# Last attention network: source logits of all heads transposed once and spread by identity columns

## What is computed

```python
ft = jnp.einsum('nhd,od->nho', hv, W)
a1 = jnp.sum(ft * attn_l, axis=-1)          # source logits, [1250, 12]
a2 = jnp.sum(ft * attn_r, axis=-1)          # destination logits
e = jax.nn.leaky_relu(a1[src] + a2[dst], negative_slope=0.2)
m = jax.ops.segment_max(e, dst, num_segments=n)
w = jnp.exp(e - m[dst])
denom = jax.ops.segment_sum(w, dst, num_segments=n)
alpha = w / jnp.maximum(denom[dst], 1e-16)
agg = jax.ops.segment_sum(alpha[:, :, None] * ft[src], dst, num_segments=n)
out = jax.nn.relu((agg + res).reshape(n, H * DOUT))
```

## Time and profile before

| what | value |
|---|---|
| median of three runs | 3462.98 us |
| lowest and highest run | 3449.34 and 3463.35 us |
| profiled execution, its own time | 3472.38 us |
| its span | 3470.6 us |
| PE busy, DVE busy, ACT busy in it | 3244.2, 2175.4, 1338.4 us |
| mean granted clock of PE | 0.951 of full speed |
| the last network, from the barrier to the end | about 3007 to 3470.6 us |

### The profile page before, as it was taken

One profiled execution on the slowest core, in us unless ns is written; L12 is line 12 of the kernel. 1 busy time (PEld: TensorE's weight loads), 2 busy tenths in 40 slices (PEclk: granted clock), 3 DMA queues, 4 the chain that ended last, 5 costly groups with the idle time before them and its releaser, 6 DMA issues. The chain is left out here.

```text
span 3470.6 us, 60801 instructions
## 1 busy us (share of the span) xinstructions
PE 3244.2 (93%) x20813; PEld 3037.5 (88%) x20813; DVE 2175.4 (63%) x4032; ACT 1338.4 (39%) x2526; POOL 944.3 (27%) x968
## 2 busy tenths in 40 slices
PE   6998998999998999999999999999998898899998
PEld 5887777888887999999997889999988686799998
DVE  6888646667677631018867601228877565499998
ACT  1245233323333121115446411124446330488885
POOL 1101733544555330005547300014546200000000
PEclk9988999999999999999998999999999889899997
DMA  3123344223222343337767633347767400300001
GB/s 80 35 81 117 121 123 117 59 73 104 55 56 67 85 135 121 102 126 244 238 208 229 177 123 101 101 143 243 242 199 233 143 33 15 73 1 0 0 0 45
DMA packets 160165, 386.02 MB, mean 111 GB/s; under 512 B 29619, under 2 KB 98784, under 8 KB 159959
## 3 DMA queue, kind: packets, MB, share of 16 engines
q0 software_dynamic: 47200, 173.39, 16.4%
q1 hardware_dynamic: 75274, 147.18, 14.4%
q10 hardware_dynamic: 37484, 62.75, 5.8%
HBM read 283.93 MB, written 99.32 MB: 110 GB/s over the span
## 5 line engine op out<-in xcount | busy, mean ns | idle before, releaser
L1846 PE MATMUL bank<-w_hi,xT_hi 128*125 128x384 f32 x1920 | 652.7, 340 | 8.0 <-ACT arena L1547 8.0
L1847 PE MATMUL bank<-w_lo,xT_hi 128*125 128x384 f32 x1920 | 650.6, 339 | 0.0
L1848 PE MATMUL bank<-w_hi,xT_lo 128*125 128x384 f32 x1920 | 650.6, 339 | 0.0
L1547 ACT COPY arena<-bank 125x384 f32<-125x384 f32 x320 | 153.7, 480 | 799.7 <-PE bank L1848 730.6
L821 POOL DMA_INDIRECT arena<-y_early,edges x204 | 233.9, 1147 | 818.0 <-issue 366.9
L895 DVE SCALAR_TENSOR_TENSOR row_lo<-arena,edges,row_hi 128x768 fp32r<-128x768 f32 x300 | 304.4, 1015 | 123.9 <-ACT row_hi L864 71.6
L2316 DVE CAST w_hi<-w_raw 128x2304 fp32r<-128x2304 f32 x35 | 47.7, 1362 | 530.3 <-PE bank L1848 524.3
L1846 PEld LDWEIGHTS bank<-w_hi,xT_hi 128*125 128x125 f32 x1920 | 358.2, 187 | 8.9 <-DVE w_lo L2317 4.6
L1847 PEld LDWEIGHTS bank<-w_lo,xT_hi 128*125 128x125 f32 x1920 | 358.0, 186 | 0.1
L1848 PEld LDWEIGHTS bank<-w_hi,xT_lo 128*125 128x125 f32 x1920 | 357.8, 186 | 0.1
L734 ACT ACTIVATE arena<-arena,low 125x1250 f32<-125x1250 f32 x170 | 227.7, 1340 | 333.6 <-DVE low L746 333.6
(11 more groups left out here) (356 smaller groups left out, 6659.3 us busy)
## 6 DMA issues: line engine op xcount, KB each, us to landing
y_early<-arena SPq DMA_DIRECT2D x200, 187.5 KB
w_raw<-in_L_gnn_W_dram ACTq DMA_DIRECT2D x30, 1152.0 KB
arena<-own_mask_d SPq DMA_DIRECT2D x50, 585.9 KB
y_late<-arena SPq DMA_DIRECT2D x120, 187.5 KB
h_d<-arena ACTq DMA_DIRECT2D x40, 250.0 KB
arena<-in_L_gnn_W_dram SPq DMA_DIRECT2D x5, 1536.0 KB, 11.9
arena<-h_d ACTq DMA_DIRECT2D x30, 250.0 KB
wadj_d<-arena SPq DMA_DIRECT2D x10, 625.0 KB
```

Of the source, the lines that this page charges most:

```text
L1846: pe.matmul(b, xT_hi[:, k, v], w_hi[:, h, k], start=(k == 0), stop=False)
L1847: pe.matmul(b, xT_hi[:, k, v], w_lo[:, h, k], start=False, stop=False)
L1848: ins = pe.matmul(b, xT_lo[:, k, v], w_hi[:, h, k], start=False, stop=(k == KD - 1))
```

## The change

PE now turns the source logits of each of the 12 heads once, at the start of the last network: 12 transposes of ten columns each, into banks 0 to 2. ACT copies them times -1 in six copies of 10 x 250 into `alT3`, even heads into the first 750 columns of `iota_row`, odd heads into the space of the old ring. A spread is then a matmul of an identity column of ten rows, repeated 125 times, by 10 x 125 of `alT3`. The diagonals on DVE, their ring and the semaphore `diag_made` are gone from this network. Number and place of the spreads stay.

```diff
-        s_diag3 = cut(rest + NT * N + node + 2 * NT * H3 + 4 * N, 4, P + 3, parts=P)[:, :, 0:P]
+        alT3 = [iota_row[0:NT, 0:H3 // 2 * P].rearrange("p (i n) -> p i n", n=P),
+                cut(rest + NT * N + node + 2 * NT * H3 + 4 * N, H3 // 2, P, parts=NT)]
+        assert NT * N + node + 2 * NT * H3 + 4 * N + H3 // 2 * P <= REST
...
-        def dve_diag(dve, v, ring, sd, als):
-
-            dve.wait_ge(s_spread, unit(v - ring))
-            dve.tensor_scalar(sd, ident[0:P, 0:P], als, -1.0, op0=ALU.mult, op1=ALU.mult).then_inc(diag_made, 1)
-
-        def pe_spread(pe, v, t, b0, sd):
-            pe.wait_ge(diag_made, v + (1 - V3))
-            pe.matmul(bank[b0 + t // 4][0:P, (t % 4) * P:(t % 4 + 1) * P], ones[0:P, 0:P], sd, start=True, stop=True).then_inc(s_spread, 1)
+        def pe_spread(pe, t, q, i, b0):
+            pe.matmul(bank[b0 + t // 4][0:P, (t % 4) * P:(t % 4 + 1) * P], ident[0:NT, t:t + 1].to_broadcast([NT, P]),
+                      alT3[q][:, bass.ds(i, 1)].rearrange("p o n -> p (o n)"), start=True, stop=True).then_inc(s_spread, 1)
...
             for c in range(3):
+                act.wait_ge(al_turned, H0 + 2 + c)
+                for q in range(2):
+                    ins = act.activation(alT3[q][:, 2 * c:2 * c + 2], bank[c][0:NT, 0:4 * P].rearrange("p (i q n) -> p i q n", q=2, n=P)[:, :, q], ACT.Copy, scale=-1.0)
+                ins.then_inc(al_ready, 1)
+            for c in range(3):
                 ins = act_spread(act, V3, c, 5, s_row3[:, 0], s_low3[:, 0])
...
             next_phase(pe)
+            for h in range(H3):
+                ins = pe.transpose(bank[h // 4][0:NT, h % 4 * P:(h % 4 + 1) * P], al3[:, 0, :, h], ident[0:P, 0:P])
+                if h % 4 == 3:
+                    ins.then_inc(al_turned, 1)
+            pe.wait_ge(al_ready, H0 + 2)
             for t in range(NT):
-                pe_spread(pe, V3 + t, t, 5, s_diag3[:, t % 4])
+                pe_spread(pe, t, 0, 0, 5)
+            pe.wait_ge(al_ready, H0 + 4)
             pe_unit_turn(pe, V3, score3[:, 0])
...
-                            pe_spread(pe, u + ((q + 1) * NT + t), t, 5, s_diag3[:, ((q + 1) * NT + t) % 4])
+                            pe_spread(pe, t, 1 - q, i + q, 5)
...
-            def diag_3(v, k, h, t):
-                dve_diag(dve, v, 4, s_diag3[:, k % 4], al3[:, 0, t, bass.ds(h, 1)])
-
...
-            for t in range(NT):
-                diag_3(V3 + t, t, 0, t)
             mask_3(V3, 0, 0)
...
                     def between():
-                        then = rden_3(u + (k + 1), k + 1) if k + 1 < PAIR or not last else None
-                        if d < NT // 2 and (q == 0 or not last):
-
-                            for t in (2 * d, 2 * d + 1):
-                                n = (q + 1) * NT + t
-                                diag_3(u + n, n, i * 2 + (q + 1), t)
-                        return then
+                        return rden_3(u + (k + 1), k + 1) if k + 1 < PAIR or not last else None
```

## The result

The changed kernel takes **3482.73 us** in the median of 16 runs (3465.43 to 3512.75); the kernel before takes 3460.7 in the median of 16 beside them (3449.34 to 3494.22). The ratio is 1.0072, 95% interval 1.0049 to 1.0096: slower by about 25 us, where +22.4 was forecast. Lines have moved: the sum is L773 now, the turn L756, the spread L784, the masks L742 and L748, DVE's normalisation L2513.

The account below looks back on a forecast made before the run. PE was taken to bound the loop; 0 for the diagonals + 20.9 for visits + 1.5 for the start = +22.4 us on 3463.0, so 3485.4 us. Its own range was 3479.1 to 3490.3; the stated range, 3463 to 3496.

Parts of the forecast that it names:

- What bounds: Last network's loop: PE 34.9 us a head against DVE 34.4, so PE bounds and removing diagonals gains 0.
- Rival 2: Last network's loop: DVE was the true bound, so 7.2 us come off, against 1.5; 3457.3 us; chance 0.03.
- The edges: Loop's spread visits: going to ten-row matmuls and back costs PE 0.38 us a visit, 55 visits, 20.9 us.
- The likeliest case: Whole kernel: PE pays at the loop's visits and at the start, +22.4 us, 3485.4 us; chance 0.78.
- the round with 34 rows: Four matmuls at 211 us, one with 34 rows: 0.32 us for going and coming, 17.6 over 55 visits.
- rival 1: Loop's visits: switching row counts costs nothing, only the start is left; 3464.5 us; chance 0.15.
- Rival 3: Loop's visits: switching costs more, as if twice 0.38 us, +41.8 + 1.5; 3506.3 us; chance 0.04.
- The start: Last network's opening: twelve transposes and six copies delay the first mask by 1.5 us, between 0 and +2.7.
- The ramp: Behind the last network's opening: work shifts against the moment PE's clock rises; taken at 0, +-1.5 us.

Follow-up runs that it names:

- rows125: The changed kernel with each spread of the last network contracted over 125 rows instead of ten; 3468.04 us, ratio 0.9999 to the kernel before.
- one_visit: The changed kernel with all ten spreads of the next head in one visit instead of five; 3537.78 us, ratio 1.0192 to the kernel before.
- two second profiles: The changed kernel and the kernel before, each unaltered and profiled once more; 3483.78 and 3483.53 us, one time each.
- rows65: The changed kernel with its spreads over 65 contraction rows instead of ten; 3498.84 us, one execution.
- block: The changed kernel with GpSimd writing block-diagonal logits, spread by three wide matmuls a head over 125 rows; 3479.58 us, ratio 1.0032 to the kernel before.

## Why the prediction was right

**What bounds.** "PE bounds the loop, by 0.5 us a head" held: without diagonals, rows125 keeps PE's step of 3.71 us and comes to 448.7 us at full clock against 448.6, where DVE as the bound would have given 7.2 us. Rival 2 is out.

**The edges.** The likeliest case came true, at its lower bound. The prediction took 0.38 us a visit from the first network, with 0.32 as the lower bound from the round with 34 rows; the loop shows 0.33. So 18.2 us in place of 20.9. The prediction expected about 0.19 on each side of the pair; it is 0.62 - 0.49 = 0.13 in the visit and 1.28 - 1.09 = 0.19 in what follows. That is not far above 0.29, the point from which rival 1 would have decided. Its evidence, the old rate inside a burst, is true (0.114 us a record) and says nothing of the edge. The bound from the earlier trace rows turned out to be the better value, though its matmuls are unlike these; the 0.38 came from a piece whose neighbours are a transposition and a matmul of 512 columns. Rival 3, twice the cost, is out for five visits a head, but the one_visit run shows that something worse than either price was near: a longer visit loses the clock.

**The start.** "+1.5 us" was wrong in size. Against the profile of before it is 6.65 - 6.41 = +0.24, with most spreads at half clock in both; in the two second profiles, with the clock at full until the spreads are done, 5.76 against 5.16, +0.60. The step that failed: the transposes were put at 3007.4 in the time of before, behind the barrier as DVE passes it. PE passes it earlier, and its transposes start 0.57 us after the start of DVE's last copy, where the first spread used to start 1.37 after it, since that one had to wait for a diagonal. So the first spread comes 1.94 us after the copy, 0.57 later than before, not 1.2, and from it to the mask it is 4.71 us, not 5.04. The bounds, 0 to +2.7, held it.

**The ramp.** "0, +-1.5" was right on average and far too narrow for one execution: the rise comes 12 to 68 us behind the first mask, in kernels with and without ten-row matmuls, and each microsecond of it costs half. This, with a like scatter in the earlier stages (M lies between 3003 and 3024 us), is most of why 16 runs of one kernel spread over 47 us: span times what the clock lacks to full is 135 us in the fastest of them and 169 in the slowest. The median of 16 against 16, +22.0 us by the two medians, is no finer than that allows; the full-clock lengths, +17.9, are. The means over the runs differ by 19.2 us against the 63 runs of before, and by 24.1 against the 16. With the start the terms that were measured add up to 17.9 + 0.6 = 18.5 us. So the mechanism was right and the sum about 4 us too large; that the two medians lie just 22.0 apart, next to the forecast's 22.4, is in part luck.

## What to carry to other kernels

Count visits, not matmuls, when a matmul of 64 or fewer contraction rows is put among full ones: each visit cost 0.33 us of the engine that bounds here, and padding the operands with zeros to more than 64 rows (65 and 125 were tried) made it free. Gathering all spreads of a head in one visit was no way out, since the clock fell behind it. Read the price at an edge from the nearest neighbours (first start to next start across the visit), not from the rate within a burst. When executions of one kernel differ by more than the effect, take out the clock: note when it rises, and compare lengths at full clock.

## What was not expected of the hardware

- In the loop of one_visit the granted clock falls from 2.4 to 1.2 GHz behind every burst of twenty ten-row records, for 10.2 to 20.5 us (3108.9 to 3129.3 in the rows shown), with PE busy all the time; behind the same burst with 125 rows it does not. In the first network it fell behind one such burst of four. The Trainium skill, "TensorE: Matmul & The Clock Gate", Part 1, ties the clock to how busy the engine has been; here "busy" as the profile reckons it, 100%, does not decide, and in this loop the rows do. How the chip reckons isn't shown.
- The clock can stay at half for over 50 us of gapless work (3020 to 3079 in the change, 3030 to 3082 in rows65, which has no matmul of 64 or fewer rows there), and in another execution of the change rise at 3022.
- The price of the small form is a step between 64 and 65 rows. Ten and 64 rows cost the same.
- An f32 matmul of 500 columns takes 0.445 us per record where one of 125 takes 0.109: wide f32 matmuls save nothing per column. The rounded records of 512 columns in the first network take 0.23 us.
- A multiplication on GpSimd of 10 x 1250 values stretched a DVE instruction that ran beside it from 1.45 to 3.17 us (block, ten heads of ten).
